# One transformer layer on one core: V one pair of score passes later in its beat, and VectorE's row-number copy ahead of its wait in the expert loop

## The chip, the core and the metric

The kernel runs on one core of one Trainium2 chip. The core has five engines with queues of their own that meet only in semaphores: TensorE (PE in the profile, with its weight loads shown apart as PEld), VectorE (DVE), ScalarE (ACT), GpSimd (POOL) and SyncE (SP, which here only issues transfers). Each engine works off its queue in order. The metric is the device time of one launch in microseconds (us), less is better; of several runs the median counts.

## What is computed

One layer of a transformer on x of 8 batches x 512 tokens x 128 numbers, all in 32-bit floats: attention with 16 heads of 8 numbers each, then a mixture of 8 experts of which each token takes the best 2.

```
x = x + attention(layernorm(x))            # 16 heads, softmax over 512 keys
t = layernorm(x)
logits = t @ Wr.T + br ; top 2 of 8 experts, weights = softmax of the two logits
o_e = relu(t @ W1[e].T + b1[e]) @ W2[e].T + b2[e]      # hidden width 512
x = x + layernorm(t + sum over the two experts of weight * o_e) * gamma + beta
```

## The kernel before

The program is one long software pipeline on all engines and then a loop.

**Attention.** The work is cut into beats T. Beat T computes, for four heads and 128 tokens, four score passes (`scores`, line 977: queries down, keys across, for the row maxima that line 770 takes on VectorE) and four transposed score passes (`scores_t`, line 993: for the exponential that line 651 takes on ScalarE), the latter six beats behind. They go in pairs: one pass of each kind sits in each pair, on different rows of the array, and both run at once. Both kinds rotate through 3 banks of PSUM, so pass k has to wait until the maximum (or the exponential) of pass k-3 is done. `values` (line 1063) closes the beat with the products with V of the beat eight before. A batch has 16 beats.

**Side tasks.** In given beats TensorE puts a side task between the second and the third pair: turning x, projections K, Q and V, the turned output and so on. All side tasks share one bank, `side_psum`, so each waits (`side_done`) until the one before it has been read out. Q of the next batch is in beat 6 of a batch: ScalarE reads it (line 619) between its third and fourth exponential, and VectorE (line 777) after its four maxima. V is in beat 7: its first two token tiles between the pairs, its last two (`second_half`) after the fourth pair, ahead of `values`. ScalarE copies V out (line 626) after its fourth exponential of the beat. In TensorE's `beat` the pairs are called 0 to 3 here.

**The expert stage.** Tokens are sent by expert to a table in DRAM with GpSimd's indirect transfers. A lot is 384 rows (three thirds of 128) of one expert. The first lot of each expert ("early", lines 1183 to 1247) is written out; the others run in a loop (17 turns in this execution, called lots 0 to 16). A lot on TensorE: 12 products for the hidden layer (lines 1541 to 1543), three transposes of the next lot (1531), and 3 x 8 short passes for the three thirds of y (1550). The third h=2 shares a bank with h=0 and so waits for the sum of h=0; h=0 of the next lot waits for the sum of h=2. On VectorE each lot takes the row numbers of the lot after next (1448), the low part of the next lot's x (1443), and then for each third: sum with the bias `ysum` (1459), which frees TensorE's bank, a copy of the row numbers to `goal_now` (1463), and `res` (1465), the weighted row. Both of the latter feed the indirect store by GpSimd (1385); so `goal_now` and `res` of a third may be written only once the store of the same third of the lot before has landed (`rows_stored[h]`). GpSimd's queue holds the 24 early stores (1247) ahead of those of the loop.

Of the kernel before, what the change touches and what calls it, by code (L numbers as in the profile page):

```python
# [47 lines left out]
GOALS = 4  # L48
# [43 lines left out]
def early_tasks(T):  # L92

    if (q := per_quad(T, 4)) is not None:
        yield "SHIFT", q
    if (q := per_quad(T, 13)) is not None:
        yield "TURN", q
    for kind, offset in (("XT", -14), ("K", -13), ("Q", -10), ("V", 7), ("OT", 26), ("O", 27), ("X2T", 31)):
        if (b := once(T, offset)) is not None:
            yield kind, b  # L100
    if T == 10:
        yield "B1", 0
# [129 lines left out]
def attention(nc, ctx, until_sorted, x, Wq, bq, Wk, bk, Wv, bv, Wo, bo, Wr, br, W1, b1, W2, beta, kept, sent, parts):  # L232
# [715 lines left out]
    def tensor(pe, early):  # L948
# [18 lines left out]
        def scores(T, g):  # L967
            n = scores_of(T)
            if n is None:
                return  # L970
            k, b, c = 4 * n + g, n // GROUPS, (n // 4) % QUADS
            if n % 4 == 0 and g == 0:
                pe.wait_ge(kq_in[c], 16 * KQ_LOADS * (b + 1))
            if k >= S_BANKS:
                pe.wait_ge(max_done, k - S_BANKS + 1)
            rows = slice(64 * (g // 2), 64 * (g // 2) + 64)
            mm(s_psum[:, k % S_BANKS, :], qs[rows, c, P * (n % 4):P * (n % 4) + P], ks[rows, c, g, :],  # L977
               start=True, stop=True).then_inc(s_made, 1)

        def scores_t(T, i):  # L980
            n = st_of(T)
            if n is None:
                return
            k, q, c, g = 4 * n + i, n // 4, (n // 4) % QUADS, (i + 2) % 4
            if n % 4 == 0 and i == 0:
                pe.wait_ge(shift_in, 16 * (q + 1))
            if k == 0:
                pe.wait_ge(w_high, 2 * E)
                pe.wait_ge(w_low, E)
            if k >= ST_BANKS:  # L990
                pe.wait_ge(exp_done, k - ST_BANKS + 1)
            rows = slice(64 * (g // 2), 64 * (g // 2) + 64)
            mm(st_psum[:, k % ST_BANKS, :], ks[rows, c, g, P * (n % 4):P * (n % 4) + P], qs[rows, c, :],  # L993
               start=True, stop=True).then_inc(st_made, 1)
# [72 lines left out]
        def beat(T):  # L1067
            scores(T, 0)
            scores_t(T, 0)
            scores(T, 1)  # L1070
            scores_t(T, 1)
            for kind, of in early_tasks(T):
                side(kind, of)
            scores_t(T, 2)
            scores(T, 2)
            scores_t(T, 3)
            scores(T, 3)
            for kind, of in early_tasks(T):
                second_half(kind, of)
            values(T)  # L1080
            if T == LAST + 31:
                early.hidden(pe, 1, 0, 2)
            for kind, of in late_tasks(T):
                side(kind, of)
            if T == -9:
                columns()

            for n in expert_weights(T):
                if n == 0:
                    pe.wait_ge(cols_ready, 1)  # L1090
                if n % E == 0:
                    pe.wait_ge((w1_loaded, w2_loaded)[n // E], 16)
                if n >= ST_BANKS:
                    pe.wait_ge(w_high, n - ST_BANKS + 1)
                    pe.wait_ge(w_low, min(n - ST_BANKS + 1, E))
                for c in range(FC):
                    src = w1raw[:, FC * n + c, :] if n < E else w2raw[:, n - E, P * c:P * c + P]
                    ins = nc.tensor.transpose(weights_bank(n)[:, P * c:P * c + P], src, ident[:])
                ins.then_inc(turned, 1)
# [157 lines left out]
def experts(nc, ctx, gamma, b2, kept, sent, results, unread, out):  # L1257
# [18 lines left out]
    goals = sb("goals", [P, GOALS, HALVES, 2], U32)  # L1276
# [5 lines left out]
    goal_now = sb("goal_now", [P, HALVES], U32)  # L1282
# [25 lines left out]
    rows_stored = [sem(f"rows_stored{h}") for h in range(HALVES)]  # L1308
# [28 lines left out]
    def stored_count(lots):  # L1337

        return lots * 16 + 16
# [97 lines left out]
    def vector(dve):  # L1437
        nc.vector.memset(marks[:, 2:3], 0.0).then_inc(y_summed, HALVES)
        turns, first = counts_of("vector", dve)

        def split_low(count):
            dve.wait_ge(xh_done, count)
            nc.vector.tensor_tensor(xl[:], x_psum[:, 0, 0:SLOTS], xh[:].bitcast(F32), ALU.subtract)\  # L1443
                .then_inc(xl_done, 1)

        def take_goals(v):
            dve.wait_ge(lot_loaded, v * 16 + 16)
            nc.vector.tensor_copy(goals[:, ds(v & (GOALS - 1), 1)],
                                  lot[:, :, D:D + 2].bitcast(U32).unsqueeze(1)).then_inc(goals_taken, 1)

        for e in range(E):
            if e == 0:
                dve.wait_ge(b2_loaded, 16 * 2)
            with dve.Fori(first[e], first[e + 1]) as u:
                take_goals(u + 1)
                split_low(u + 2)
                for h in range(HALVES):
                    dve.wait_ge(y_made, u * HALVES + h + 1)
                    nc.vector.tensor_tensor(ysum[:, h, :], y_at(h), b2b[:, e, :], ALU.add)\  # L1459
                        .then_inc(y_summed, 1)  # L1460
                    dve.wait_ge(rows_stored[h], stored_count(u))
                    dve.wait_ge(y_summed, u * HALVES + HALVES + h + 1)
                    nc.vector.tensor_copy(goal_now[:, h:h + 1], goals[:, u & (GOALS - 1), h, 0:1])\
                        .then_inc(y_done, 1)
                    nc.vector.tensor_scalar(res[:, h, :], ysum[:, h, :],  # L1465
                                            goals[:, u & (GOALS - 1), h, 1:2].bitcast(F32), None,
                                            ALU.mult).then_inc(y_done, 1)

        def sum_first():
            dve.wait_ge(got_in[0], 32)
            nc.vector.tensor_tensor(z[:, 0], got[:, 0, tiles(0), :], got[:, 1, tiles(0), :], ALU.add).then_inc(z_done, 1)
            dve.wait_ge(z_done, 1)
            nc.vector.tensor_tensor(z[:, 1], z[:, 0], kept.xn2[:, tiles(0), :], ALU.add).then_inc(z_done, 1)
            dve.wait_ge(z_done, 2)

        def combine(b):
            if b == 0:  # L1480
                sum_first()
            else:
                dve.wait_ge(z1_done, b)
            for j in range(TILES):
                ins = nc.vector.bn_stats(stats3[:, b, j, :], sum_of(b, j))
            ins.then_inc(s3_done, 1)
            dve.wait_ge(s3_done, b + 1)
            for j in range(TILES):
                ins = nc.vector.bn_aggr(moments3[:, b, j, :], stats3[:, b, j, :])
            ins.then_inc(m3_done, 1)  # L1490

        def complete(b):
            dve.wait_ge(n_done, b + 1)
            at = tiles(b)
            nc.vector.tensor_tensor(normed[:, b], normed[:, b],
                                    gammab[:].unsqueeze(1).to_broadcast([P, TILES, D]), ALU.mult).then_inc(g_done, 1)
            dve.wait_ge(g_done, b + 1)
            nc.vector.tensor_tensor(got[:, 0, at, :], normed[:, b], kept.xres[:, at, :], ALU.add).then_inc(fin_done, 1)

        def complete_last(b):  # L1500
            dve.wait_ge(v3_done, b * 2 + 2)
            for j in range(TILES):
                ins = nc.vector.scalar_tensor_tensor(
                    out=normed[:, b, j, :], in0=sum_of(b, j), scalar=minus_mean[:, b, j:j + 1],
                    in1=gammab[:], op0=ALU.add, op1=ALU.mult)
            ins.then_inc(g_done, 1)
            dve.wait_ge(r3_done, b + 1)
            dve.wait_ge(g_done, b + 1)
            at = TILES * b
            for j in range(TILES):  # L1510
                ins = nc.vector.scalar_tensor_tensor(
                    out=got[:, 0, at + j, :], in0=normed[:, b, j, :], scalar=rstd3[:, b, j:j + 1],
                    in1=kept.xres[:, at + j, :], op0=ALU.mult, op1=ALU.add)
            ins.then_inc(fin_done, 1)

        for b in range(B):
            combine(b)
            if b >= COMPLETE_LAG:
                complete(b - COMPLETE_LAG)
        for b in range(B - COMPLETE_LAG, B - 1):  # L1520
            complete(b)
        complete_last(B - 1)
# [74 lines left out]
```

## Time and profile before

| | us |
|---|---|
| median of 3 runs | 641.54 |
| lowest and highest | 640.49, 642.63 |
| the profiled execution, its own time | 643.3 |
| its span, first to last instruction | 641.5 |
| PE busy | 591.1 (92%) |
| DVE busy | 485.6 (76%) |
| ACT busy | 436.5 (68%) |
| POOL busy | 232.7 (36%) |

The profile shows one execution. The attention pipeline fills it to about 470 us, the early lots go to 515, the loop to 607, and the rest adds up, normalises and stores. Busy shares are means over these stages; the chain of work that ended last tells what sets the time in each.

### The profile page before, as it was taken

To read this page: it belongs to the slowest core of one execution; us is meant where nothing else is said; L and a number is where in the kernel's file an instruction comes from. 1 tells how busy PE (TensorE), PEld (TensorE's weight loads), DVE (VectorE), ACT (ScalarE), POOL (GpSimd) and SP (SyncE) were. 2 spreads that over 40 slices of the span, in tenths; PEclk is the share of its full clock that TensorE was granted. 3 is DMA by queue.
4 is the path that set the end of the run, shared out by engine and by line. 5 is a ranking of instruction groups with operands and counts; after the bars stand their busy time and mean duration, and the time that the engine had idled before them with its cause. 6 is when DMAs were issued, how large, how long until landed. Compare 5 with 4: busy or idle time off the path is not lost.

```text
span 641.5 us, 12423 instructions
## 1 busy us (share of the span) xinstructions
PE 591.1 (92%) x3656; PEld 321.8 (50%) x3656; DVE 485.6 (76%) x1287; ACT 436.5 (68%) x886; POOL 232.7 (36%) x397
## 2 busy tenths in 40 slices
PE   2889999999999999999999999999989999999972
PEld 1634333443443343334334344343389999999730
DVE  3577898999899899899899989988246444555358
ACT  2634787788788888888878888778755544444323
POOL 7110010031422412512332142142177775655545
PEclk9965999999999999999999999999989999999987
DMA  6751812213312411331231230113012432222172
GB/s 196 258 161 50 179 45 80 77 34 94 108 28 77 121 40 48 95 91 31 89 97 39 88 110 27 33 54 103 33 44 73 136 91 68 76 75 79 33 278 114
DMA packets 46621, 56.97 MB, mean 89 GB/s; under 512 B 8366, under 2 KB 25818, under 8 KB 46564
## 3 DMA queue, kind: packets, MB, share of 16 engines
q1 hardware_dynamic: 40580, 45.06, 24.5%
q0 software_dynamic: 4544, 8.53, 3.9%
q10 hardware_dynamic: 1440, 2.69, 1.1%
q8 instruction: 27, 0.44, 0.3%
q14 instruction: 30, 0.25, 0.1%
HBM read 29.28 MB, written 27.16 MB: 88 GB/s over the span
## 4 chain that ended last, share of the span: by engine, by line
PE 64%; DVE 21%; ACT 8%; issue 4%; DMA 2%; POOL 1%; DVEq 0%; ACTq 0%; POOLq 0%
PE pv_psum L1063 13%; DVE mneg L770 11%; PE st_psum L993 10%; PE s_psum L977 10%; PE y_psum L1550 6%; ACT pt L651 4%; PE y_psum L1230 3%; PE side_psum L999 3%; PE side_psum L1025 2%; PE side_psum L1019 2%; ACT xn L669 2%; PE h_psum L1541 2%; PE h_psum L1543 2%; PE h_psum L1542 2%; DVE split L777 2%
## 5 line engine op out<-in xcount | busy, mean ns | idle before, releaser
L770 DVE TENSOR_REDUCE mneg<-s_psum 128x1 f32<-128x512 f32 x512 | 322.9, 684 | 31.9 <-PE s_psum L977 30.4
L651 ACT ACTIVATE pt<-st_psum 128x512 f32<-128x512 f32 x512 | 279.1, 598 | 68.6 <-PE st_psum L993 63.4
L977 PE MATMUL s_psum<-ks,qs 64*128 64x512 f32 x512 | 203.9, 472 | 3.2 <-DVE mneg L770 2.0
L993 PE MATMUL st_psum<-qs,ks 64*128 64x512 f32 x512 | 194.3, 458 | 7.7 <-ACT pt L651 7.6
L977 PEld LDWEIGHTS s_psum<-ks,qs 64*128 64x128 f32 x512 | 83.1, 190 | 109.6 <-DVE mneg L770 87.8
L1063 PE MATMUL pv_psum<-pt,vst 128*16 128x512 f32 x1024 | 135.1, 601 | 0.0
L993 PEld LDWEIGHTS st_psum<-qs,ks 64*128 64x128 f32 x512 | 79.9, 187 | 51.8 <-ACT pt L651 41.3
L1418 ACT ACTIVATE hid<-h_psum,b1c 128x384 f32<-128x384 f32 x68 | 36.9, 581 | 45.9 <-PE h_psum L1543 45.9
L1385 POOL DMA_INDIRECT results<-res,goal_now x51 | 49.9, 979 | 34.5 <-DVE res L1465 22.9
L510 POOL DMA_INDIRECT sent<-xrow,placeu x56 | 54.5, 974 | 16.3 <-issue 16.3
L1550 PE MATMUL y_psum<-w2t,hid 128*128 128x128 f32 x408 | 48.7, 276 | 1.1 <-DVE ysum L1459 1.1
L1550 PEld LDWEIGHTS y_psum<-w2t,hid 128*128 128x128 f32 x408 | 47.0, 192 | 1.5 <-DVE ysum L1459 0.8
L460 POOL TENSOR_TENSOR vareps<-moments,eps 128x4 f32<-128x4 f32 x8 | 1.6, 200 | 95.3 <-DVE moments L740 95.3
L1063 PEld LDWEIGHTS pv_psum<-pt,vst 128*16 128x16 f32 x1024 | 17.0, 94 | 35.6 <-ACT pt L651 25.8
L521 POOL TENSOR_TENSOR start<-fill,zero_e 128x8 f32<-128x8 f32 x8 | 1.6, 204 | 89.7 <-DVE counts L815 89.7
L554 POOL TENSOR_TENSOR vareps<-moments,eps 128x4 f32<-128x4 f32 x8 | 1.6, 198 | 88.6 <-DVE moments L851 88.6
L1219 ACT ACTIVATE hid<-h_psum,b1c 128x384 f32<-128x384 f32 x32 | 17.5, 581 | 19.7 <-PE h_psum L1214 19.6
L643 ACT COPY pvs<-pv_psum 128x512 f32<-128x512 f32 x32 | 18.8, 589 | 11.2 <-PE pv_psum L1063 11.0
L1247 POOL DMA_INDIRECT results<-early_res,early x24 | 23.6, 982 | 7.2 <-issue 5.3
L1541 PE MATMUL h_psum<-xh,w1h 128*128 128x384 f32 x68 | 24.4, 359 | 0.0
L1443 DVE TENSOR_TENSOR xl<-x_psum,xh 128x384 fp32r<-128x384 f32 x17 | 9.5, 557 | 19.4 <-ACT xh L1412 19.4
L1025 PE MATMUL side_psum<-xt,wt 128*128 128x512 f32 x32 | 21.8, 769 | 2.4 <-DVE split L777 1.6
(219 smaller groups left out, 807.5 us busy)
## 6 DMA issues: line engine op xcount, KB each, us to landing
parts<-split SPq DMA_DIRECT2D x48, 256.0 KB, 3.0
ks<-parts SPq DMA_DIRECT2D x128, 48.0 KB
qs<-parts SPq DMA_DIRECT2D x128, 48.0 KB
lot<-sent SPq DMA_DIRECT2D x18, 198.0 KB
sent<-tail SPq DMA_DIRECT2D x16, 198.0 KB, 5.3
xres<-in_L_attn_x_dram SPq DMA_DIRECT2D x8, 256.0 KB, 3.5
pt<-in_L_ffn_W_dram SPq DMA_DIRECT2D x1, 2048.0 KB, 14.4
got<-results SPq DMA_DIRECT2D x8, 256.0 KB, 6.6
```

What stands on the lines that cost most here:

```text
L510: nc.gpsimd.indirect_dma_start(out=sent, out_offset=bass.IndirectOffsetOnAxis(ap=placeu[:, b // (B - 1), j, k:k + 1], axis=0), in_=xrow_of ...
L651: nc.scalar.activation(pt[:, n % PT_SLOTS, (g + 2) % 4, :], st_psum[:, k % ST_BANKS, :], ACT.Exp, scale=SCALE).then_inc(exp_done, 1)
L770: nc.vector.tensor_reduce(mneg[:, (n // 4) % 2, at:at + 1], s_psum[:, k % S_BANKS, :], AX_X, ALU.max, negate=True).then_inc(max_done, 1)
L977: mm(s_psum[:, k % S_BANKS, :], qs[rows, c, P * (n % 4):P * (n % 4) + P], ks[rows, c, g, :], start=True, stop=True).then_inc(s_made, 1)
L993: mm(st_psum[:, k % ST_BANKS, :], ks[rows, c, g, P * (n % 4):P * (n % 4) + P], qs[rows, c, :], start=True, stop=True).then_inc(st_made, 1)
L1025: ins = mm(bank, wt[:, "KQ".index(kind), :], xt[:, of % 2], start=True, stop=True)
L1063: ins = mm(pv_psum[32 * g:32 * g + 16, 0, :], vst[:, b % 2, n % 4, 4 * (q % QUADS) + g, :], pt[:, n % PT_SLOTS, g, :], start=(n % 4 == 0), ...
L1247: self.nc.gpsimd.indirect_dma_start(out=self.results, out_offset=bass.IndirectOffsetOnAxis(ap=self.kept.early[:, n, h, D:D + 1].bitcast(U3 ...
L1385: nc.gpsimd.indirect_dma_start(out=results, out_offset=bass.IndirectOffsetOnAxis(ap=goal_now[:, h:h + 1], axis=0), in_=res[:, h, :], in_of ...
L1418: nc.scalar.activation(hid[:, f, :], h_psum[:, f, 0:SLOTS], ACT.Relu, bias=b1c[:, FC * e + f:FC * e + f + 1]).then_inc(relu_act, 1)
L1541: mm(dst, w1h[:, k, :], xh[:], start=True, stop=False)
L1550: ins = mm(y_at(h), hid[:, f, P * h:P * h + P], w2t[:, FC * e + f, :], start=(f == 0), stop=(f == FC - 1))
```

## The change

Two edits. In TensorE's `beat`, side tasks other than V stay between pairs 1 and 2, while V moves behind pair 2, so that it stands between pairs 2 and 3. Only beat 7 of each batch (8 beats in all) is touched, and no other side task is in it. V's second half, ScalarE's and VectorE's order stay.

In VectorE's loop, the wait for `rows_stored[h]` and the copy to `goal_now` move from behind `ysum` to ahead of the wait for y; `res` stays behind `ysum`. No instruction is added or removed.

```diff
@@ -1070,9 +1070,13 @@
             scores(T, 1)
             scores_t(T, 1)
             for kind, of in early_tasks(T):
-                side(kind, of)
+                if kind != "V":
+                    side(kind, of)
             scores_t(T, 2)
             scores(T, 2)
+            for kind, of in early_tasks(T):
+                if kind == "V":
+                    side(kind, of)
             scores_t(T, 3)
             scores(T, 3)
@@ -1455,13 +1459,13 @@
                 for h in range(HALVES):
+                    dve.wait_ge(rows_stored[h], stored_count(u))
+                    nc.vector.tensor_copy(goal_now[:, h:h + 1], goals[:, u & (GOALS - 1), h, 0:1])\
+                        .then_inc(y_done, 1)
                     dve.wait_ge(y_made, u * HALVES + h + 1)
                     nc.vector.tensor_tensor(ysum[:, h, :], y_at(h), b2b[:, e, :], ALU.add)\
                         .then_inc(y_summed, 1)
-                    dve.wait_ge(rows_stored[h], stored_count(u))
                     dve.wait_ge(y_summed, u * HALVES + HALVES + h + 1)
-                    nc.vector.tensor_copy(goal_now[:, h:h + 1], goals[:, u & (GOALS - 1), h, 0:1])\
-                        .then_inc(y_done, 1)
                     nc.vector.tensor_scalar(res[:, h, :], ysum[:, h, :],
```

## Rows read from the trace of the kernel before

**Rows 1.** Page: shares of the chain that ended last; TensorE's clock in tenths.
```profile
PEclk9965999999999999999999999999989999999987
...
PE 64%; DVE 21%; ACT 8%; issue 4%; DMA 2%; POOL 1%; DVEq 0%; ACTq 0%; POOLq 0%
```

**Rows 2.** Timeline, PE, fourth batch's V beat: start, length, engine, line, out<-in, [idle<-releaser].
```profile
211.44 0.39 PE L977 MATMUL s_psum<-ks,qs 64*128 64x512 f32 x1
...
212.03 0.71 PE L999 MATMUL side_psum<-wt,xt 128*128 128x128 f32 x4 [0.19 <-DVE split L777]
212.67 0.50 PE L993 MATMUL st_psum<-qs,ks 64*128 64x512 f32 x1
...
213.97 1.05 PE L1063 MATMUL pv_psum<-pt,vst 128*16 128x512 f32 x8
```

**Rows 3.** Timeline, DVE (two lines) and ACT (one), the same beat.
```profile
211.23 0.74 DVE L777 SCALAR_TENSOR_TENSOR split<-side_psum,bcols,split 128x512 fp32r<-128x512 f32 x1
...
211.96 2.57 DVE L770 TENSOR_REDUCE mneg<-s_psum 128x1 f32<-128x512 f32 x4
...
211.05 1.70 ACT L651 ACTIVATE pt<-st_psum 128x512 f32<-128x512 f32 x3
```

**Rows 4.** Chain that ended last, the same beat: start, length, what.
```profile
212.74 0.43 PE st_psum L993
```

**Rows 5.** Timeline, PE, a beat without side task, pairs 1 and 2.
```profile
233.60 0.39 PE L977 MATMUL s_psum<-ks,qs 64*128 64x512 f32 x1
...
233.84 0.39 PE L977 MATMUL s_psum<-ks,qs 64*128 64x512 f32 x1
```

**Rows 6.** Timeline, PE, V beat of the first batch.
```profile
57.79 1.23 PE L999 MATMUL side_psum<-wt,xt 128*128 128x128 f32 x4 [0.46 <-DVE split L777]
```

**Rows 7.** Tile goal_now: waits before it (us, times), and landing of the stores.
```profile
  DMA results<-res,goal_now: 9.0, 11
...
DMA to landing us min/median/max: 2.1/2.2/4.5
```

**Rows 8.** Timeline, PE, DVE and POOL, the last lot of the loop.
```profile
601.22 2.85 PE L1550 MATMUL y_psum<-w2t,hid 128*128 128x128 f32 x24
...
602.07 0.56 DVE L1443 TENSOR_TENSOR xl<-x_psum,xh 128x384 fp32r<-128x384 f32 x1 [1.57 <-ACT xh L1412]
602.55 0.28 DVE L1459 TENSOR_TENSOR ysum<-y_psum,b2b 128x128 f32<-128x128 f32 x1
603.06 0.15 DVE L1463 COPY goal_now<-goals 128x1 uint32 x1 [0.23 <-DVE ysum L1459]
603.20 0.29 DVE L1465 TENSOR_SCALAR res<-ysum,goals 128x128 f32<-128x128 f32 x1
...
604.34 0.98 POOL L1385 DMA_INDIRECT results<-res,goal_now  x1 [1.62 <-DVE res L1465]
```

**Rows 9.** Timeline, PE, the loop's lots 1 to 3.
```profile
522.42 2.84 PE L1550 MATMUL y_psum<-w2t,hid 128*128 128x128 f32 x24
...
528.21 2.05 PE L1550 MATMUL y_psum<-w2t,hid 128*128 128x128 f32 x16 [0.49 <-DVE ysum L1459]
...
530.85 1.16 PE L1550 MATMUL y_psum<-w2t,hid 128*128 128x128 f32 x8 [0.60 <-DVE ysum L1459]
531.76 0.42 PE L1541 MATMUL h_psum<-xh,w1h 128*128 128x384 f32 x1
...
534.29 2.84 PE L1550 MATMUL y_psum<-w2t,hid 128*128 128x128 f32 x24
```

**Rows 10.** Timeline, DVE and POOL, the loop's lots 0 to 2.
```profile
526.27 0.15 DVE L1463 COPY goal_now<-goals 128x1 uint32 x1 [2.23 <-DMA results<-res,goal_now]
...
528.72 0.15 DVE L1463 COPY goal_now<-goals 128x1 uint32 x1 [0.65 <-DMA results<-res,goal_now]
...
530.52 0.28 DVE L1459 TENSOR_TENSOR ysum<-y_psum,b2b 128x128 f32<-128x128 f32 x1
...
523.71 0.98 POOL L1385 DMA_INDIRECT results<-res,goal_now  x1 [0.30 <-issue]
```

## Prediction, made before the changed kernel was run

> **What bounds the kernel now.** I read first the page's chain of what ended last, then that chain in order of time, then the timelines of the two places that the change touches. TensorE carries 64% of the chain, VectorE 21% [rows 1]. So an edit is worth what it does to TensorE's next start, and in two places that is decided by VectorE. The first is the V beat. Pair 1 starts at 211.44; V does not follow it, but stands until 212.03, because `side_psum` is still being read by VectorE's low part of Q (`split`, 211.23 to 211.97) [rows 2, 3]. The chain runs through that wait. The second is the expert loop. A lot is bound by TensorE, whose passes lie back to back, except in lots 1 and 2, where TensorE stands before 528.21 and before 530.85 for `ysum` [rows 9]; the root of both is VectorE, which at 526.27 comes out of 2.23 us of waiting for the landing of lot 0's store, issued at 523.71 behind the early stores [rows 10]. The tail behind the last lot is a chain of stores on GpSimd.
>
> **Part A, V behind pair 2.** Removed is nothing; the order becomes pairs 0, 1, 2, V, pair 3, V's second half. Is pair 2 free to run at once? Its maxima bank needs the fourth maximum of the beat before, which stands ahead of `split` in VectorE's queue, done by 211.3. Its other bank needs the fourth exponential of the beat before, the first of the three at 211.05, so done at 211.05 + 0.60 = 211.65 and seen about 211.69 [rows 3]. A third pair in a run follows the second after 0.23 to 0.24 [rows 5]: 211.44 + 0.23 = 211.67. So pair 2 starts at about 211.69 instead of 212.67. V then starts between 212.03 (its own wait) and 212.69 less what a pair takes: 211.69 + 0.43 = 212.12, if the pair's weight load is exposed as in a pair that starts a run [rows 4]. I take 212.08. V's half takes 212.67 - 212.03 = 0.64 [rows 2]. Pair 3 needs the first maximum of this beat (211.96 + 0.64 = 212.60, seen 212.64 [rows 3]), which is in time for 212.72. But it now stands alone and pays the exposed load: 0.43 [rows 4] where the second of two pays 0.23. So `values` starts at 212.08 + 0.64 + 0.43 + 0.64 = 213.79 instead of 213.97 [rows 2]: a gain of 0.18, with bounds 0.13 (V at 212.12) and 0.23 (V at 212.03). The full stall of about 0.26 does not come back, since breaking up a run of two pairs costs 0.2 of load time and joining three saves most, not all, of it. What is late next? ScalarE and VectorE in this beat get their pass earlier and idle after the beat; no maximum starts before 211.96 anyway, so four of them still end at 214.53 [rows 3], and TensorE needs them later than that only for the next beat's SHIFT, a microsecond on. Everything that follows hangs on the same chain, so I count the gain whole.
>
> It holds in the six middle batches, which show the same pattern (stalls of 0.19 to 0.20 in each; the row stands for six). In the first batch the clock is at half speed, tenths 5 [rows 1], and V stands 0.46 [rows 6]; but there the exponential that pair 2 needs comes out at about 57.4, late too, and the pair costs twice as much: 0, bounds -0.1 and +0.3. In the last batch there is no Q in front of V, so V has no stall that could go: 0. Sum A: 6 x 0.18 = **-1.1**, bounds -0.8 and -1.4.
>
> Here the Trainium skill says more: "TensorE: Matmul & The Clock Gate", section "Step-by-step: what each phase is for", has weight loads pulled ahead of matmuls in flight where row groups don't conflict or the background buffer is used. By that the lone pair 3 would not pay its 0.2 and A would be six times about 0.27, -1.6. The rows show a pair behind V paying it (0.43 [rows 4]), so the sum goes by the row.
>
> **Part B, the copy ahead of the wait.** VectorE does the same work; its order per third changes from sum, copy, row to copy, sum, row. What queues behind the moved wait is now `ysum`, and TensorE waits for `ysum`.
>
> B1, *lots 1 and 2.* Before, the sum of h=0 of lot 1 was made ahead of the wait for the store, so TensorE ran on to 528.21. Now that sum stands behind it: copy at 526.27 (the landing does not move, the store is bound by GpSimd's queue), sum 0.14 later, at 526.41, done 526.69, seen by TensorE 0.04 later (530.52 + 0.28 against 530.85 [rows 9, 10]), at 526.73. TensorE's third h=2 of lot 1, due at 522.42 + 16 x 0.112 = 524.21, starts then; from such a start to the next lot is 531.76 - 530.85 = 0.91 [rows 9], so lot 2 starts at 527.64. Its y is due 2.53 later (534.29 - 531.76 [rows 9]), at 530.17; the sum of h=2 of lot 1 is ready, since its copy starts at 528.72 [rows 10] and ends it at 529.1. Its h=2 is due at 531.96. VectorE's low part comes 0.85 after y (602.07 - 601.22), the copy 0.48 later, the sum 0.14 after that [rows 8]: 531.64, seen 531.96. Lot 3 thus starts at 532.86 instead of 531.76 [rows 9]: a loss of **+1.1**. The stall at 530.85 goes, but the one at 524.2 that takes its place is larger. The bound below is 0.9; above it is 2.1, if the store of h=0 of lot 1 (on GpSimd at 527.1 + 0.85 = 527.98) takes the slowest landing, 4.5 instead of 2.2 [rows 7]: then the copy waits to 532.5.
>
> B2, *every lot.* The copy of h=0 now stands between `xl` and the first sum. How much later is the sum? Nearest row: from the start of a copy to the start of the next instruction is 603.20 - 603.06 = 0.14 (0.135 in finer readings) [rows 8]. VectorE's sequencer must also work out the row's address first, but it has the 0.48 us that `xl` takes for that. So the sum ends at 602.55 + 0.135 + 0.28 = 602.97, seen 603.01, and TensorE's h=2 is due at 601.22 + 16 x 0.112 = 603.01 [rows 8]. The cover is just used up. A third that starts at its release costs 0.91 to the next lot against 0.90 in the row; I take 0.02 per lot, 17 x 0.02 = **+0.3**. Bounds: 0, and 0.1 per lot (the sequencer needing one more address step) = 1.7. All 17 lots show the same 1.33 from y to the first sum except the disturbed lot 2. Waits for landings at h=1 and h=2 (11 waits, 9.0 us, of which 2.23 is the one at h=0 of lot 1 [rows 7, 10]) now also hold the sum of their own third, but these have 2 us of slack until the next lot's y.
>
> The Trainium skill speaks for a smaller price: "VectorE: DVE Perf Modes", section "The TRN2 errata — SBUF-src ops pay a fixed extra latency per instruction", gives 58 cycles plus the elements at 0.96 GHz, for this copy an estimated 0.06 us. By it the sum would keep 0.07 of cover, B2 would be 0 and the whole 0.3 less. The row has 0.15 for the copy and 0.14 to the next start, and the measurement decides.
>
> B3, *the end.* In the last lot `res` starts 0.14 after the sum's end instead of behind the copy: 602.69 + 0.28 + 0.14 = 603.11 instead of 603.20. GpSimd's three stores follow from `res` of h=0 (604.34 [rows 8]), each 1.28 behind the last [rows 10], so the tail gains **-0.1** (bounds 0, -0.2).
>
> **Sum.** -1.1 + 1.1 + 0.3 - 0.1 = +0.2 on a span of 641.5. The profiled execution took 643.3 by its own time, 1.8 of it outside the span, which the change doesn't touch, and 1.8 above the median; the difference is put on the median: 641.54 + 0.2 = **641.7**.
>
> **Rivals.**
> 1. *The wait in the V beat is only replaced.* Pair 2 meets the exponential or pair 3 the first maximum, or the lone load eats it all. The margins are 0.02 and 0.08. A is 0: 642.8.
> 2. *Slower: the first sum falls behind in every lot.* Place: the copy of h=0 between `xl` and `ysum`. Price: what it delays beyond 0.14 of cover, 17 times. If address steps and the copy come one after the other (0.135 + 0.2), the stall is 0.2 a lot: 641.7 - 0.3 + 3.4 = 644.8. It decides from 0.13 us per lot on, or with less if stores of h=0 land late: they have 3.3 us, the median is 2.2, the slowest 4.5 [rows 7].
> 3. *Faster: B1 doesn't cost.* If in this execution the early stores' backlog is shorter, copy 526.27 comes sooner and A stands alone: 641.54 - 1.1 - 0.1 + 0.3 = 640.6. Against it: the stores are 0.98 + 0.30 = 1.28 apart, with nothing but issue between them [rows 10].
> 4. *The change doesn't do what it says*, TensorE's V waiting for the same in the same place: ruled out for `split`, which ends before pair 2 would.
>
> **Chances.** Forecast 0.60 (its own range 640.8 to 643.5); rival 1 0.15; rival 2 0.13; rival 3 0.12. The range 640.2 to 644.0 leaves out about 2 in 10. About 0.3%, 1.9 us, is what a measurement can tell. Faster by more (below 639.6): 0.05; slower by more (above 643.5): 0.14; within: 0.81.
>
> **What would show it.** In the V beats of the middle batches, V's wait for `split` gone or below 0.1, `values` 0.13 to 0.23 sooner after pair 0, each batch shorter by as much. In lot 1, one stall of about 2.5 us ahead of h=2, and lots 0 to 3 1.1 us longer; in the steady lots, y to first sum 1.46 instead of 1.33, and lots of 5.13 to 5.15 us. Wrong would be: V beats unchanged, a lot above 5.2, h=0 waiting for landings in lots beyond 1, or a batch that loses the gain in a later beat.

## The result, and the profile after

| | before | changed |
|---|---|---|
| median | 641.32 us (6 runs) | 645.85 us (6 runs) |
| lowest and highest | 639.96, 642.63 | 645.20, 648.78 |
| ratio | | 1.0067, 95% interval 1.0044 to 1.0091 |
| the profiled execution, own time | 643.3 | 645.71 |
| its span | 641.5 | 644.0 |

The changed kernel is slower by some 4.5 us, outside the predicted range. In two later series it was 1.0036 [1.0002, 1.0069] and 1.0043 [1.0022, 1.0064], with medians of 645.65 and 645.67 us; all in all its 25 runs have a median of 645.7, but six of them lie between 639.7 and 642.1. That spread turned out to be part of the answer. Executions in which TensorE's clock was lower as a whole are left out of every median, ratio and table here, except that the profile of the changed kernel with a shortened queue is of such an execution, of which only the loop is read, where the clock was full.

**The V beat.** TensorE's timeline of the changed kernel in the fourth batch's V beat answers to [rows 2] (start, length, engine, line, operation):

```profile
210.84 0.49 PE L977 MATMUL s_psum<-ks,qs 64*128 64x512 f32 x1
...
211.17 0.39 PE L977 MATMUL s_psum<-ks,qs 64*128 64x512 f32 x1
...
211.44 0.49 PE L977 MATMUL s_psum<-ks,qs 64*128 64x512 f32 x1
211.87 0.71 PE L999 MATMUL side_psum<-wt,xt 128*128 128x128 f32 x4
212.51 0.49 PE L993 MATMUL st_psum<-qs,ks 64*128 64x512 f32 x1
...
212.93 0.71 PE L999 MATMUL side_psum<-wt,xt 128*128 128x128 f32 x4
213.57 1.05 PE L1063 MATMUL pv_psum<-pt,vst 128*16 128x512 f32 x8
```

Pairs 0, 1 and 2 follow one another, V comes behind pair 2 with no wait for `split`, and the lone pair 3 takes 0.42 (212.51 to 212.93). From pair 1 to `values` it is 2.40 us, where [rows 2] have 213.97 - 211.44 = 2.53: a gain of 0.13 per beat. With the batches numbered from 0, it was 310.33 us from the `values` of batch 1's V beat to that of batch 7 and is 309.69 (109.96 to 419.65). That distance holds five of the six beats that gain, 5 x 0.13 = 0.65.

**The loop's lots 1 and 2.** TensorE and then VectorE, to be held against [rows 9] and [rows 10]:

```profile
521.15 1.95 PE L1554 MATMUL y_psum<-w2t,hid 128*128 128x128 f32 x16
525.43 2.08 PE L1554 MATMUL y_psum<-w2t,hid 128*128 128x128 f32 x8 [2.33 <-DVE ysum L1466]
527.16 0.67 PE L1545 MATMUL h_psum<-xh,w1h 128*128 128x384 f32 x1
527.63 0.52 PE L1546 MATMUL h_psum<-xl,w1h 128*128 128x384 f32 x1
527.95 0.52 PE L1547 MATMUL h_psum<-xh,w1l 128*128 128x384 f32 x1
...
529.03 0.34 PE L1545 MATMUL h_psum<-xh,w1h 128*128 128x384 f32 x1
529.21 0.34 PE L1546 MATMUL h_psum<-xl,w1h 128*128 128x384 f32 x1
```
```profile
524.96 0.15 DVE L1463 COPY goal_now<-goals 128x1 uint32 x1 [2.40 <-DMA results<-res,goal_now]
525.09 0.29 DVE L1466 TENSOR_TENSOR ysum<-y_psum,b2b 128x128 f32<-128x128 f32 x1
...
526.15 0.29 DVE L1466 TENSOR_TENSOR ysum<-y_psum,b2b 128x128 f32<-128x128 f32 x1
...
527.32 0.15 DVE L1463 COPY goal_now<-goals 128x1 uint32 x1 [0.44 <-DMA results<-res,goal_now]
```

VectorE waits 2.40 us for the landing as before, but the first sum now stands behind that wait, and TensorE stands 2.33 us before h=2. The two stalls of [rows 9] (0.49 and 0.60) are gone. This is the replacement that was predicted: h=2 was due at 521.15 + 16 x 0.112 = 522.94 and starts 2.49 later, where 526.73 - 524.21 = 2.52 was worked out. (The 2.33 of the line is TensorE's idle time alone.) What was not predicted is in the lengths: the eight passes of h=2 take 2.08 instead of 1.16, and the hidden passes follow each other 0.32 apart (527.63, 527.95) where they are later 0.18 apart (529.03, 529.21). The view by windows (busy time of PE, PEld, DVE, ACT and POOL, then TensorE's granted clock, DMA share, GB/s) says why:

```profile
core 0: us, PE busy (x) PEld busy (x) DVE busy (x) ACT busy (x) POOL busy (x), PEclk, DMA share, GB/s
520.00:524.00 4.00, 3.10 (x25) 2.88 (x23) 0.72 (x2) 1.98 (x5) 3.09 (x4) 1.00 0.37 107
524.00:526.00 2.00, 0.57 (x2) 0.57 (x3) 0.87 (x3) 0.00 (x0) 1.63 (x2) 0.84 0.13 51
526.00:529.00 3.00, 3.00 (x14) 3.00 (x13) 1.42 (x6) 0.49 (x1) 1.85 (x2) 0.54 0.11 44
529.00:532.00 3.00, 3.00 (x26) 2.97 (x25) 0.89 (x4) 2.09 (x5) 1.10 (x2) 1.00 0.17 43
```

Behind the stall the granted clock is at its lower level, 1.2 GHz, for 3.4 us (means of 0.84 over 2 us and 0.54 over 3 us make 0.64 + 2.76), and TensorE works that time at half speed.

**A steady lot.** TensorE, its weight loads (PEld) and VectorE; the last line has the loads of the lot of [rows 8], in the kernel before:

```profile
535.58 2.89 PE L1554 MATMUL y_psum<-w2t,hid 128*128 128x128 f32 x24
535.48 2.80 PEld L1554 LDWEIGHTS y_psum<-w2t,hid 128*128 128x128 f32 x24
536.44 0.56 DVE L1447 TENSOR_TENSOR xl<-x_psum,xh 128x384 fp32r<-128x384 f32 x1 [1.43 <-ACT xh L1416]
536.91 0.14 DVE L1463 COPY goal_now<-goals 128x1 uint32 x1
536.97 0.28 DVE L1466 TENSOR_TENSOR ysum<-y_psum,b2b 128x128 f32<-128x128 f32 x1
...
601.11 2.76 PEld L1550 LDWEIGHTS y_psum<-w2t,hid 128*128 128x128 f32 x24
```

From y to the first sum it is 1.39 us (1.33 in [rows 8]), the 24 passes take 2.88 to 2.89 instead of 2.84 or 2.85, and most lots take 5.17 instead of 5.13 (the longest undisturbed ones 5.25 instead of 5.19). One late lot shows a landing wait at h=0 that reaches TensorE, and it takes 5.79. The store that it waits for, its copy, and TensorE:

```profile
575.08 0.98 POOL L1389 DMA_INDIRECT results<-res,goal_now  x1 [0.93 <-DVE res L1469]
...
578.99 0.15 DVE L1463 COPY goal_now<-goals 128x1 uint32 x1 [0.47 <-DMA results<-res,goal_now]
...
579.45 1.16 PE L1554 MATMUL y_psum<-w2t,hid 128*128 128x128 f32 x8 [0.40 <-DVE ysum L1466]
```

The waits on landed stores are, for `goal_now`, against [rows 7]:

```profile
  DMA results<-res,goal_now: 11.3, 15
...
DMA to landing us min/median/max: 2.1/2.2/3.1
```

**Where the loop's time went.** The starts of the three x transposes mark the lots; from those of the last early lot to those of the loop's last lot there are 17 distances. The first five hold the stall of lot 1. The kernels in the table are told of in the next section.

| kernel | first five | other twelve | sum | clock fell at lot 1 |
|---|---|---|---|---|
| before | 27.32 | 61.73 | 89.05 | no |
| changed, first series | 29.95 | 62.94 | 92.89 | yes |
| changed, second | 28.56 | 63.15 | 91.71 | no |
| changed, third | 28.48 | 62.86 | 91.34 | no |
| loop edit alone | 29.94 | 62.70 | 92.64 | yes |
| loop edit at h=0 alone | 28.40 | 62.35 | 90.75 | no |
| changed, TensorE kept busy in lot 1, each of two | 28.4 | 62.4 | 90.76 | no |

So three separate amounts can be read: +1.1 in lots 1 to 3 from the stall itself, +1.4 to 1.5 more when the clock falls behind it, and about +0.6 (0.05 a lot) in the other twelve. On top comes one lot with a late landing at h=0, 0.4 to 0.8 us in the three profiles of the changed kernel and the one of the loop edit alone. The two profiles with TensorE kept busy have no such landing; one of their lots is 0.2 longer because TensorE's first hidden product starts 0.2 late, with no wait for a store.

### The profile page after: what moved, and what is told of

Read it like the earlier page. It is cut to its first block, busy times and chain, and to the rows that moved or that the text cites. A ratio compares the mean times of both kernels' runs of the same rounds, so it can differ in the third digit from the quotient of the medians.

```text
span 644.0 us, 12423 instructions
## 1 busy us (share of the span) xinstructions
PE 591.9 (92%) x3656; PEld 322.6 (50%) x3656; DVE 484.7 (75%) x1287; ACT 437.1 (68%) x886; POOL 232.7 (36%) x397
## 4 chain that ended last, share of the span: by engine, by line
PE 64%; DVE 18%; ACT 8%; issue 4%; POOL 3%; DMA 2%; SPq 0%; DVEq 0%; ACTq 0%; POOLq 0%
PE pv_psum L1063 13%; PE st_psum L993 10%; PE s_psum L977 10%; DVE mneg L770 9%; PE y_psum L1554 7%; ACT pt L651 4%; PE y_psum L1234 3%; PE side_psum L1025 2%; PE side_psum L999 2%; PE side_psum L1019 2%; PE h_psum L1545 2%; PE h_psum L1546 2%; PE h_psum L1547 2%; ACT xn L669 2%; PE side_psum L1042 1%
## 5 line engine op out<-in xcount | busy, mean ns | idle before, releaser
L1554 PE MATMUL y_psum<-w2t,hid 128*128 128x128 f32 x408 | 50.4, 280 | 2.7 <-DVE ysum L1466 2.7
L1554 PEld LDWEIGHTS y_psum<-w2t,hid 128*128 128x128 f32 x408 | 48.5, 194 | 3.1 <-DVE ysum L1466 3.1
```

The lines of the kernel that those rows point to most:

```text
L1554: ins = mm(y_at(h), hid[:, f, P * h:P * h + P], w2t[:, FC * e + f, :], start=(f == 0), stop=(f == FC - 1))
```

## The experiments

**The two edits apart.** First the V edit without the loop edit.

```diff
             for kind, of in early_tasks(T):
-                side(kind, of)
+                if kind != "V":
+                    side(kind, of)
             scores_t(T, 2)
             scores(T, 2)
+            for kind, of in early_tasks(T):
+                if kind == "V":
+                    side(kind, of)
```

> Part A alone: V one pair later, the loop as before. Theory 1 (part A gives what its traces show, all the loss is in the loop): the V beats of the six middle batches 0.14 us shorter each, the attention stage 0.8 us shorter, the loop as before with lots of 5.13 us, a ratio to the kernel before of 0.998 to 0.9995. Theory 2 (part A costs something that the traces of one execution hide, as a fall of TensorE's clock elsewhere): ratio of 1.001 or more, while the V beats are shorter.

Measured: 639.2 us, ratio 0.9962 [0.9942, 0.9982], more than the 0.998 that theory 1 had as its lowest. From the `values` of batch 1 to that of batch 7 it has 309.67 us against 310.33 before; its loop takes 89.08. The V edit is a gain, and this is the fastest kernel of the study; how much of its 2 us is the edit is taken up below, under "All runs by their clock".

Then the loop edit without the V edit.

```diff
+                    dve.wait_ge(rows_stored[h], stored_count(u))
+                    nc.vector.tensor_copy(goal_now[:, h:h + 1], goals[:, u & (GOALS - 1), h, 0:1])\
+                        .then_inc(y_done, 1)
                     dve.wait_ge(y_made, u * HALVES + h + 1)
...
-                    dve.wait_ge(rows_stored[h], stored_count(u))
                     dve.wait_ge(y_summed, u * HALVES + HALVES + h + 1)
-                    nc.vector.tensor_copy(goal_now[:, h:h + 1], goals[:, u & (GOALS - 1), h, 0:1])\
-                        .then_inc(y_done, 1)
```

> Part B alone: the wait and the copy ahead of the sum in all three thirds, V as before. Theory 1: the whole loss and a little more, ratio 1.0075 to 1.0095 (4.8 to 6 us), of it about 2.5 us from lot 1's stall, 1.5 us from TensorE's clock at half level behind it, 0.6 us from 0.04 us in each steady lot. Theory 2: ratio 1.003 to 1.005, the rest of the measured loss being part A's.

Measured: 645.75 us over five runs, 1.0061 [1.0041, 1.0080], less than theory 1 expected and more than theory 2. The whole loss is in the loop edit. Its profile shows in lot 1 the same picture as the changed kernel, the lower clock included:

```profile
523.68 2.07 PE L1550 MATMUL y_psum<-w2t,hid 128*128 128x128 f32 x8 [2.25 <-DVE ysum L1462]
```

**Which third.** The loop edit for the second and third of the thirds, and for the first alone:

```diff
+                    if h > 0:
+                        dve.wait_ge(rows_stored[h], stored_count(u))
+                        nc.vector.tensor_copy(goal_now[:, h:h + 1], goals[:, u & (GOALS - 1), h, 0:1])\
+                            .then_inc(y_done, 1)
                     dve.wait_ge(y_made, u * HALVES + h + 1)
...
-                    dve.wait_ge(rows_stored[h], stored_count(u))
+                    if not (h > 0):
+                        dve.wait_ge(rows_stored[h], stored_count(u))
...
```

> Part B for h=1 and h=2 only; in h=0 the wait and the copy stay behind the sum. Theory 1 (the loss comes from h=0, whose sum has no slack): lots steady at 5.13 us, TensorE does not stand before the third h=2 of lot 1; its wait before lot 2's y grows from 0.5 to about 1.5 us; ratio 1.0005 to 1.002. Rival (what costs is VectorE's order as such, in all thirds): two thirds of the loss, ratio 1.005.

```diff
+                    if h == 0:
...
+                    if not (h == 0):
...
```

> Part B for h=0 only. Theory 1: nearly all the loss of part B, ratio 1.006 to 1.009, with the stall of about 2.5 us in lot 1, TensorE's clock at half level behind it and lots of 5.17 us. Rival (all thirds alike): a third of the loss, ratio 1.002 to 1.003.

Measured: h=1 and 2 alone 641.62 us, 0.9990 [0.9973, 1.0008]; h=0 alone 643.93 us, 1.0037 [1.0012, 1.0062]. Both are less than expected, the second by far (1.006 at least was expected; its profile has no fall of the clock). The first has steady lots of 5.13 us and a loop of 89.41, although its copies wait for landings 16 times for 11.8 us together, and its stall for a store sits where it was, behind the sum of h=0:

```profile
518.98 0.28 DVE L1463 TENSOR_TENSOR ysum<-y_psum,b2b 128x128 f32<-128x128 f32 x1
521.38 0.15 DVE L1467 COPY goal_now<-goals 128x1 uint32 x1 [2.13 <-DMA results<-res,goal_now]
```

The second has the stall, steady lots of 5.17 and a loop of 90.75 (+1.7). So h=0 makes most of the loss, by a wait and by a copy in front of the one sum that TensorE needs soon. This profile has no landing wait at h=0 beyond lot 1. In these profiles late landings there came only where the copies of h=1 and 2 wait ahead of their sums as well, but not in all of those: four have one, and three (the two with TensorE kept busy and the one with the shortened queue) have none.

**Does the clock fall each time?** The changed kernel again, in one series with a version in which TensorE has something to do in the stall: three long passes ahead of the wait before h=2 of lot 1, into a bank that nobody reads. (The piece of the loop with number 1 is lot 1 alone.) It computes the whole output.

> The changed kernel as it is, as the partner of the next run on the same chip. Theory 1 (the missing term of the forecast is TensorE's clock, which falls to half level in or behind the 2.4 us stall of lot 1): the stall is there again; where the clock falls, lot 1 to lot 2 takes 9.2 to 9.3 us, where it does not, 7.7 us.

```diff
-        for e in range(E):
-            with pe.Fori(first[e], first[e + 1]) as u:
+        pieces = [(0, first[0], 1), (0, 1, first[1])] + [(e, first[e], first[e + 1]) for e in range(1, E)]
+        for piece, (e, start, end) in enumerate(pieces):
+            with pe.Fori(start, end) as u:
...
+                    if piece == 1 and h == Y_BANKS:
+                        for _ in range(3):
+                            mm(idle_psum[:, 0, :], ident[:], w2t[:, 0:FC, :].rearrange("p c d -> p (c d)"),
+                               start=True, stop=True)
```

> The changed kernel with three passes of 128x512 to a bank that nobody reads, put in front of the wait of h=2 in lot 1 (and only there, the first expert's second lot): some 1.8 us of work inside the stall of 2.3 us, so that TensorE stands only 0.5 us. Nothing else is changed and the landing that ends the stall comes no sooner. Theory 1 (clock): no half level in the loop, lot 1 to lot 2 takes 7.7 us instead of 9.2, about 1.5 us less in all than the changed kernel where that falls. Rival (the extra 1.5 us is the stall's own, by queues or loads behind it): 9.2 us stay. If the work did not fit into the stall, the lot would take up to 1.8 us more.

Measured: changed 645.65 us, kept busy 641.21, 1.0002 [0.9982, 1.0023]. The changed kernel's second profile has the stall, even a little longer, but no fall: h=2 takes 1.16, and the clock stays up.

```profile
521.12 1.16 PE L1554 MATMUL y_psum<-w2t,hid 128*128 128x128 f32 x8 [2.48 <-DVE ysum L1466]
```
```profile
521.00:524.00 3.00, 2.88 (x19) 2.88 (x20) 1.72 (x8) 1.16 (x3) 2.09 (x3) 1.00 0.14 57
```

The version kept busy shows its passes in the stall and no fall. They take 2.57 us there, not the 1.8 that was expected, and h=2 starts 0.2 behind the end of the sum (525.32 to 525.53):

```profile
522.96 2.74 PE L1554 MATMUL idle_psum<-w2t,ident 128*128 128x512 f32 x6
525.53 1.05 PE L1560 MATMUL y_psum<-w2t,hid 128*128 128x128 f32 x8
```
```profile
524.00:526.00 2.00, 2.00 (x9) 1.01 (x9) 0.95 (x3) 0.00 (x0) 1.67 (x2) 1.00 0.15 57
526.00:529.00 3.00, 3.00 (x23) 2.96 (x22) 1.42 (x8) 1.85 (x4) 1.81 (x2) 1.00 0.11 44
```

The extra passes free nothing and wait for nothing, and the lots behind them are nearly all as long as in the changed kernel; what differs is that TensorE is not idle, and that its loop over the first expert is written as two. A version with the split loop and without the passes was not run. To see whether this holds, both were run again in one series.

> The changed kernel with three long passes into an unread bank ahead of h=2 of lot 1, again. Theory (TensorE's clock falls in some executions in or behind the stall of lot 1, and busy passes in it prevent that): no half-level stretch between the first and the fourth lot, first five lot distances together 28.4 us; 1 to 2 us faster than the changed kernel of the same call. Rival (the clock has no part in the loss): the same time as the changed kernel within 0.5 us.

> The changed kernel once more, beside the version with TensorE kept busy. Theory (clock): 643.5 to 646 us, the profile with or without a fall of the clock behind the stall of 2.3 us in lot 1; where it falls, the first five lot distances are about 30 us together, where not, 28.5. Rival (the clock has no part): as fast as the version kept busy, and 28.5 us in either case.

Measured: kept busy 641.04 us, 0.9992 [0.9974, 1.0009]; changed 645.67, 1.0043 [1.0022, 1.0064]. Twice, then, the version with busy passes is faster by more than 4 us in the median; in the mean it is 1.7 us in the first series, whose intervals overlap, and 3.6 in the second. The third profile of the changed kernel is of a 646.44 us execution, and again its lot 1 has no fall:

```profile
526.63 1.16 PE L1554 MATMUL y_psum<-w2t,hid 128*128 128x128 f32 x8 [2.40 <-DVE ysum L1466]
```

So the fall at lot 1 is not what made this execution slow. Against the profile before (643.3 by its own time) the loop has 2.3 us more, and the stage behind the loop 1.1 more: there the lower clock lasts 6.8 us instead of 3.4. What was on record for a profile without the fall, 28.5 us for the first five, came (28.48); but the time as a whole is long all the same, which the theory of a fall at lot 1 doesn't cover.

**The backlog taken away.** The last nine early stores are moved behind the loop on GpSimd's queue, once in the kernel before and once in the changed one. All results are computed and stored; only later.

```diff
-                    for n in range(1, E):
-                        if n == TURNS_READ:
+                    for n in range(1, TURNS_READ):
+                        if n == TURNS_READ - 1:
...
+        for n in range(TURNS_READ, E):
+            for h in range(HALVES):
+                early.store(pool, n, h)
```

> The kernel before with the last 9 of the 24 early stores moved behind the loop on GpSimd (the tail grows by about 9 x 1.28 = 11.5 us, in both kernels of this pair alike). The stores of lot 0 are then not held up. All theories: TensorE's two waits in lot 2 (0.49 and 0.60 us) vanish and the 17 lots take 1.5 us less than before, 87.6 us from first to last transposes.

> The changed kernel with the same 9 stores moved behind the loop. Theory 1 (the large part of part B's loss needs the landing of lot 0's store to be late, the rest is 0.05 us per lot): no stall in lot 1, no half level, lots of 5.17 to 5.18 us; the 17 lots take 0.8 to 0.9 us more than in the partner e7, in place of 3.8. Rival (the order of VectorE's queue is what costs, whatever the landings): 2 us or more over e7.

Measured: 652.8 us, 1.0223 [1.0139, 1.0306], and 650.1 us, 1.0147 [1.0107, 1.0187], with three and four executions. Both pay for the stores at the end, which is no matter here. Between each other the changed one is not slower any more (the intervals overlap). In the loop the stall is gone in both, and so is the loss of the first lots; the 17 lots take 87.41 and 88.18 us, 0.045 a lot apart. GpSimd waits for VectorE instead of the other way round:

```profile
517.27 0.98 POOL L1385 DMA_INDIRECT results<-res,goal_now  x1 [8.57 <-DVE res L1467]
```

That shows the root of the stall, the queue of early stores [rows 10], by removing it.

**The copy's own price.** The kernel before with one more copy of one element, into a word that nobody reads, in front of the sum of h=0.

```diff
                     dve.wait_ge(y_made, u * HALVES + h + 1)
+                    if h == 0:
+                        nc.vector.tensor_copy(spare[:], gammab[:, 0:1])
                     nc.vector.tensor_tensor(ysum[:, h, :], y_at(h), b2b[:, e, :], ALU.add)\
```

> The kernel before with one more copy of one element per lot, into a word that nobody reads, right in front of the sum of h=0; the copy of the row numbers and its wait stay where they were. Theory (the copy itself costs 0.04 to 0.05 us a lot, because TensorE's weight load for h=2 has only some 0.03 us of cover left; the rest of the loss comes from the wait in lot 1): lots of 5.17 instead of 5.13 us, 17 x 0.045 = 0.8 us, ratio 1.001, no stall in lot 1 beyond that of the kernel before. Rival (the copy in front of the sum is free, the steady loss is from waiting for the store): lots of 5.13, ratio 1.000. Rival 2 (the copy is the main cost): ratio 1.003 or more.

Measured: 642.55 us, 1.0010 [0.9995, 1.0024], lots of 5.16 to 5.17 in the place of 5.13, the first five lots together 27.66 (27.32 before), the other twelve 62.44 (+0.71). The sum moves by 0.06 and the 24 passes take 2.89, as in the changed kernel:

```profile
539.29 0.14 DVE L1460 COPY spare<-gammab 128x1 f32<-128x1 f32 x1
539.35 0.28 DVE L1462 TENSOR_TENSOR ysum<-y_psum,b2b 128x128 f32<-128x128 f32 x1
```

So the whole steady loss is the copy's place, with no wait in it.

**All runs by their clock.** Each run has its mean granted clock (but for the first series of the kernel before). Over the runs of the kernels with their stores in place, times fall on lines with a common slope, 4.2 us per 0.01 of clock. A kernel's distance from the line of the kernel before is its loss at the same clock; the ± is a 95% interval:

| kernel | runs | mean clock | at the same clock, us |
|---|---|---|---|
| before | 66 | 0.9701 | 0 |
| V edit alone | 8 | 0.9717 | -1.1 ± 0.5 |
| loop edit at h=1, 2 | 9 | 0.9711 | 0.0 ± 0.5 |
| spare copy | 12 | 0.9706 | +0.6 ± 0.4 |
| loop edit at h=0 | 11 | 0.9682 | +1.8 ± 0.4 |
| loop edit alone | 5 | 0.9682 | +2.8 ± 0.6 |
| changed | 25 | 0.9670 | +1.6 ± 0.3 |
| changed, kept busy | 19 | 0.9719 | +0.4 ± 0.3 |

The changed kernel loses 1.6 us by its structure, and its mean clock is lower by 0.003, which is 1.3 us more in the mean; in the median it is more, since 11 of its 25 runs have a mean clock of at most 0.964, which none of the 66 runs of the kernel before had. The two edits add up: +2.8 for the loop edit and -1.1 for the V edit. The edit at h=0 alone has +1.8 of the +2.8; of the other 1.0 the late landing that goes with the whole loop edit is 0.4 to 0.8 in its profiles, and the intervals allow the rest.

## Why the prediction was wrong

**Part A was right in kind, a little large.** V's wait is gone, no new wait came, pair 2 started 0.27 behind pair 1 (0.25 predicted), and the lone pair pays 0.42 (0.43). V came 0.43 behind pair 2 instead of the 0.39 that I chose: of the two values the worse one, the full exposed load, holds. So 0.13 per beat, the low bound of the row-based sum, and six times that is 0.8 instead of 1.1. Rival 1 (nothing gained) falls.

The Trainium skill, "TensorE: Matmul & The Clock Gate", section "Step-by-step: what each phase is for", has weight loads pulled ahead of matmuls in flight; by that A was 1.6. The trace disagrees here: the pair that stands alone behind V takes 0.42, and V itself starts 0.43 behind its pair. The 1.6 counts only the stall that goes, about 0.27 a beat; the prediction's own rows without the lone pair's 0.2 would have given 0.18 + 0.20 = 0.38 a beat, 2.3 in all, which is further off still.

**B1 was right as a stall and incomplete as a price.** One late start of 2.49 where 2.52 was predicted, two old stalls gone, first five lots 1.1 to 1.2 longer in each profile where the clock stays up (28.40, 28.48, 28.56 against 27.32). The failed step of the prediction is a term that it put at nothing without a reason: TensorE's granted clock, taken as that of the kernel before. Over all runs its mean is 0.9670 where the kernel before has 0.9701, and 0.9648 in the six runs of the first series. One place where this shows is behind the stall of B1. In two of five profiles with that stall and nothing to fill it, the clock was at half its level for 3.4 us behind it and the five lots took 1.4 to 1.5 more. [Rows 9] had only stalls of 0.49 and 0.60 with full speed behind them. But [rows 1] have lower tenths at the start, at about 470 us and at the end, so the level does change within an execution, and the bound above should have had it.

**B2 came out of two errors that partly cancel.** I took 0.14 for the delay of the sum and 0.14 for its cover, and got 0.02. The delay is 0.06: the start of the copy to the start of the sum, 536.91 to 536.97. The 0.135 came from a copy that itself stands right behind a wait for `ysum` [rows 8]; a copy right behind `xl`, as in the new place, holds up the next start by less than half of that. And the cover was counted to the matmul, but the waiting instruction is its weight load, which runs 0.10 ahead (535.48 against 535.58). The loads follow each other 0.112 apart, so load 17 of 24 is due at 535.48 + 16 x 0.112 = 537.27. It comes at 537.31, 0.05 behind the end of the sum and 0.16 behind load 16. In the lot of [rows 8] it comes 0.07 behind the end of the sum, on time, so the cover was only some 0.01 to 0.02 before. Delay less cover leaves 0.05 a lot, by which the 24 loads take 2.80 instead of 2.76: 0.6 in twelve lots and 0.8 in seventeen, where +0.3 was the sum for all; it lies inside the bounds. The spare copy confirms it.

The Trainium skill, "VectorE: DVE Perf Modes", section "The TRN2 errata — SBUF-src ops pay a fixed extra latency per instruction", gives 58 cycles and the elements, an estimated 0.06 us for this copy. The trace agrees with that as a start-to-start distance (0.06), though the record's length says 0.14. The conclusion that I drew for that case, no loss, was still wrong, because the cover was wrong.

**A late landing at h=0** was in rival 2 as an aggravation and not in the forecast. It cost 0.6, 0.8 and 0.55 in one lot of the changed kernel's three profiles. The 3.1 us that the view gives as the slowest landing does not show it, because in this profile landings are recorded only for the stores of h=1. The store of h=0 starts at 575.08 and its copy at 578.99, 3.9 later, where in lot 1 it was 2.56 before (523.71 to 526.27) and is 2.57 (522.39 to 524.96). The slack was as counted: the copy was due 0.47 behind the start of `xl` at 577.96, which is 3.35 behind the store, and in the first profile with TensorE kept busy, with the same order on VectorE, the copy comes 3.35 behind its store (573.51 to 576.86) and waits for nothing. So the landing was slower, not the slack smaller; why it was slower in four profiles (the changed kernel's three and the loop edit alone) is open. With this and with lots of 5.22 to 5.25, two of the prediction's signs of being wrong came true: a landing wait at h=0 beyond lot 1, and lots above 5.2.

**B3 was right.** In the last lot GpSimd's first store starts 2.96 us behind y (606.71 - 603.75), where [rows 8] have 604.34 - 601.22 = 3.12: 0.16 sooner. From the last transposes to the end of the span it is 40.54 us against 40.62, -0.1.

**The sum again.** -0.8 + 1.1 + 0.6 - 0.1 and 0.6 for the late landing is +1.4, and at the same clock +1.6 ± 0.3 was measured. That would have been 643.1 us, within my range. Of the rest of the 4.5, the mean clock of the first series (0.9648 against 0.9701) is worth 2.2 us on the common line, and my forecast had nothing for it; the remaining 0.7 stays unexplained, and the clock of the six runs of the kernel before isn't on record. The nearest rival was the second: its sign and its place (h=0, in front of the first sum) were right, its price was not, 0.2 a lot from address steps where 0.05 is seen. Rival 3 is answered by the shortened queue: without the backlog B1 costs nothing, but in every profile of the changed kernel the backlog is there.

**What stays open.** It isn't known why the changed kernel's clock is lower, nor how much of that comes from lot 1. The version with busy passes is faster in both series, by 4.4 and 4.6 us in the median and by 1.7 and 3.6 in the mean. The profiles explain a part: the fall at lot 1, 1.4 us when it happens, and it happened in two of five; and the late lot, 0.4 to 0.8. But a large part of what sets two executions apart lies elsewhere, ahead of the loop. The `values` of batch 1's V beat start at 109.96, 105.53 and 110.51 us in the changed kernel's profiles and at 109.95 and 107.19 in those kept busy, mostly by the length of the early stretch at the lower clock (27.3, 17.1, 27.3; 27.3, 20.5 us). That is up to 5 us, some 400 us before lot 1 is reached. From there to the end of the span the three take 534.0, 532.4 and 534.2, the two 531.8 and 531.8, and the kernel before 531.4. So in the profiles the busy passes are worth 0.6 to 2.4 us behind that point, and no run shows whether the rest of the 4 us is more than chance in the early stage. The lower clock behind the loop lasts 6.8 us instead of 3.4 in the third profile of the changed kernel, but also in the one of the V edit alone and the one of the edit at h=0. Most executions have no profile, so in which stage they lose isn't known.

**A version that beats both** is the V edit alone: 639.2 us, 0.9962 [0.9942, 0.9982] of the kernel before. At the same clock that is 1.1 ± 0.5 us, of which the V beats show 6 x 0.13 = 0.8; the other 0.7 in the mean is that its eight runs had a mean clock of 0.9717 against 0.9701, which nothing here ties to the edit.

## What to carry to other kernels

Count cover up to the instruction that really waits: here that was the weight load, 0.1 us ahead of the matmul, and that was most of the 0.14 of cover. Never move a wait for a slow queue ahead of the one result that the busiest engine needs next, even where the queue keeps up in the steady state; look at the queue's backlog at the stage's start. When an edit makes one long stall (here 2.3 us) out of several short ones on TensorE, put the lower clock into the upper bound (1.4 us more in two of five profiles here), and compare the mean granted clock of many runs, not of one profile. Before two profiles are compared as a whole, cut them into stages: here the first 110 us alone differed by up to 5.

## What the runs showed of the hardware

- TensorE's clock fell to its lower level in or behind an idle stretch of 2.25 to 2.33 us in two profiles and not in three others with 2.29 to 2.48 us, so the length of the stall alone does not decide. Behind the fall the hidden passes were 0.32 apart instead of 0.18, for 3.4 us.
- Executions of one kernel differ in how long the lower clock holds: the early stretch was 17.1, 20.5 or 27.3 us long in different profiles, and with it batch 1's `values` stood at 105.5 to 105.9, 107.2 to 108.4 or 109.8 to 110.5; over whole runs 0.01 of mean clock is worth 4.2 us. That is as much as the edit under test; a single profile pair can't show an effect of 2 us in the whole span, but lot distances can.
- A copy of one element delays the next VectorE instruction by 0.06 us when nothing else holds that one, less than half of the record's 0.14; right behind a wait it was 0.10 to 0.14.
- A wait for VectorE's sum was paid at the weight load: it came 0.054 us behind the end of the sum when it had waited, and 0.067 when it had not.
- A score pair that follows another kind of pass took 0.42 to 0.43 us of TensorE to the next start, against 0.24 to 0.27 in a run: its weight load is exposed.
- GpSimd's indirect stores start 1.28 us apart from a full queue, and a copy that waits for one starts 2.4 to 4.7 us behind it, mostly within 3.1.
